# Two state-space layers: scans of one state and two sequences, driven from PSUM, summed by accumulating turns

## The reference

```python
x = silu(conv(in_proj_w @ hidden) + conv_b)        # u: (4, 256 channels, 256 times)
dt_low, B, C = split(x_proj_w @ u, [8, 16, 16])
delta = softplus(dt_proj_w @ dt_low + dt_proj_b)
A = -exp(A_log)                                     # (256, 16 states)
def step(state, (d, b, c, u)):                      # scan over the 256 times
    state = state * exp(d[..., None] * A) + (d * u)[..., None] * b[:, None, :]
    return state, einsum('ben,bn->be', state, c)
y = (ys + D * u) * silu(z)
return swapaxes(y, 1, 2)
```

## Time and profile before

| | |
|---|---|
| median of 3 runs | 2662.31 us (2658.98 to 2666.39) |
| the profiled execution, its own time | 2666.48 us |
| its span, first to last instruction | 2664.5 us |
| PE busy, mean granted clock | 1977.8 us (74%), 0.844 |
| DVE busy | 1610.6 us (60%) |
| ACT busy | 786.8 us (30%) |
| POOL busy | 580.7 us (22%) |
| scans of L795, 32 | 204.2 us |
| multiplications of L790, 64 | 75.2 us |

### The profile page before, as it was taken

One profiled execution on the slowest core, in us unless ns is written; L12 is line 12 of the kernel. 1 busy time (PEld: TensorE's weight loads), 2 busy tenths in 40 slices (PEclk: granted clock), 3 DMA queues, 4 the chain that ended last, 5 costly groups with the idle time before them and its releaser, 6 DMA issues.

```text
span 2664.5 us, 27749 instructions
## 1 busy us (share of the span) xinstructions
PE 1977.8 (74%) x9734; PEld 1251.4 (47%) x9734; DVE 1610.6 (60%) x2456; ACT 786.8 (30%) x1999; POOL 580.7 (22%) x327
## 2 busy tenths in 40 slices
PE   5646668746635776788888864553999999999986
PEld 3522234412222445666666633343566665555743
DVE  4279956879988543555555179998366424444114
ACT  1333302133212025455554011110355314444000
POOL 1314420014501014233332036555000000000000
PEclk9867878768867879888889877876899999999966
DMA  3000020010010210000001100000000100000000
GB/s 102 7 32 0 0 54 3 5 45 0 0 40 1 35 42 2 17 12 12 12 10 50 71 1 0 0 0 0 6 10 10 42 10 13 12 10 21 1 32 16
DMA packets 25727, 48.98 MB, mean 18 GB/s; under 512 B 6262, under 2 KB 19603, under 8 KB 24092
## 3 DMA queue, kind: packets, MB, share of 16 engines
q1 hardware_dynamic: 25644, 47.85, 5.9%
HBM read 42.20 MB, written 1.05 MB: 16 GB/s over the span
## 4 chain that ended last, share of the span: by engine, by line
PE 51%; DVE 37%; ACT 4%; issue 4%; SPq 1%; POOL 1%; DMA 1%; DVEq 0%; ACTq 0%; POOLq 0%
DVE big L795 8%; PE banks L1116 7%; PE banks L1085 7%; PE banks L1125 7%; PE banks L1054 6%; DVE big L1796 5%; PE banks L1108 3%; DVE big L1792 3%; DVE big L495 2%; PE banks L1350 2%; PE banks L417 2%; PE banks L428 2%; DVE big L790 2%; DVE big L776 1%; DVE arena L1172 1%
## 5 line engine op out<-in xcount | busy, mean ns | idle before, releaser
L1191 DVE COPY arena<-banks 128x512 f32<-128x512 f32 x196 | 135.4, 691 | 329.8 <-PE banks L1108 329.5
L218 POOL TENSOR_TENSOR ln_rstd<-ln_var_eps,neg_half 128x2 f32<-128x2 f32 x48 | 36.8, 766 | 1060.8 <-DVE ln_var_eps L206 1060.8
L1085 PE MATMUL banks<-big 128*128 128x256 f32 x784 | 235.6, 413 | 6.0 <-ACT big L1227 4.4
L1116 PE MATMUL banks<-arena,big 128*128 128x256 f32 x784 | 227.7, 414 | 6.3 <-DVE arena L1191 6.3
L1248 ACT ACTIVATE arena<-banks,arena 128x256 f32<-128x256 f32 x392 | 193.0, 499 | 60.8 <-DVE arena L1165 43.0
L795 DVE TENSOR_TENSOR_SCAN big<-big 128x2048 f32<-128x2048 f32 x32 | 204.2, 6380 | 1.1
L707 PE MATMUL banks<-big,ident 128*128 128x512 f32 x288 | 171.3, 749 | 39.2 <-POOL big L868 39.1
L868 POOL TENSOR_TENSOR big<-big 128x2048 f32<-128x2048 f32 x32 | 144.7, 4523 | 252.2 <-DVE big L795 252.2
L1266 ACT ACTIVATE big<-banks 128x256 f32 (+1 forms) x196 | 75.1, 383 | 348.4 <-PE banks L1116 348.4
L1054 PE MATMUL banks<-x_feat,arena 128*128 128x512 f32 x392 | 176.4, 592 | 0.0
L1125 PE MATMUL banks<-arena,big 128*128 128x256 f32 x784 | 174.3, 382 | 1.9 <-ACT big L1266 1.9
(11 more groups left out here) (313 smaller groups left out, 3568.1 us busy)
## 6 DMA issues: line engine op xcount, KB each, us to landing
big<-big SPq DMA_DIRECT2D x32, 64.0 KB, 2.3
arena<-in_L0f_w SPq DMA_DIRECT2D x1, 2048.0 KB, 8.0
arena<-in_L1a_wo SPq DMA_DIRECT2D x1, 2048.0 KB
arena<-in_L1f_gv SPq DMA_DIRECT2D x1, 2048.0 KB
arena<-in_L2a_qk_w SPq DMA_DIRECT2D x1, 2048.0 KB
big<-big SPq DMA_DIRECT2D x64, 32.0 KB
arena<-in_L2x_wo SPq DMA_DIRECT2D x1, 2048.0 KB
arena<-in_L2x_q_w SPq DMA_DIRECT2D x16, 128.0 KB, 2.0
```

The source lines that it names most:

```text
L1085: last = mm(ps[:, h * SEQ:(h + 1) * SEQ], q[:, b * SEQ + h * P:b * SEQ + (h + 1) * P], k[:, b * SEQ:(b + 1) * SEQ], start=True, stop=not s ...
L1116: last = mm(slot, self.v[:, 2 * b + kc, :], self.probs_t[:, u % 2, kc, :], start=(kc == 0), stop=(kc == 1))
L1191: v.tensor_copy(self.probs_t[:, u % 2].rearrange("p a b -> p (a b)"), B[4 + u % 2][:]).then_inc(self.turn_read, 1)
```

## The change

The steps of a state-space layer become 32: one state and two sequences (half the tokens) each, first the 16 states of the first half, then those of the second. They are written out, without a hardware loop.

- PE spreads B into bank 4 and C into bank 5, one bank each. It then adds by turning: eight transposes of 128 x 128 of out, accumulated in banks 6 and 7, which so hold the sum by tokens. With the last state of a half it also turns and adds D * u (sixteen transposes). In its queue, slot s holds spread(s+1) and then add(s-1).
- DVE writes drive into PSUM, banks 0 and 1 or 2 and 3 in turn, 128 x 1024, and scans 128 x 1024 with decay from SBUF and drive from PSUM. Slot s holds drive(s+1) and then scan(s).
- ACT makes the decay with two exponentials of 128 x 510, copies one bank of C, scales u by D in slot 0, and reads the two banks of sums into SBUF (over du) after each half.
- POOL multiplies 128 x 1024. It clears the decay's first times after the softplus, when du is done.
- The gate is no tile any more: the LayerNorms ahead of layers 1 and 4 (those of layers 0 and 3) apply Silu where they copied, so that x_feat holds the gate; DVE multiplies the sums by it, pair by pair, and the next LayerNorm adds from SBUF. These two LayerNorms turn into banks 0 to 3.
- The x_proj matmuls wait for both halves of u and go to banks 4 and 5; dt uses banks 6 and 7 twice.
- SmallHeads (attention of layers 0 and 6) and StateSpace get parameters hosts and room, with which an attention would carry a state-space layer's steps in its own queues. The table of makers, which the diff leaves as it is, passes neither, so hosts is False and room is None everywhere.

The diff, cut to its core (the parts under hosts and the renaming of semaphores left out):

```diff
 class LayerNorm:
+    def turn_bank(self, pair):
+        return pair if self.gates else 4 + pair
...
-            ... e.x_tok[:, ts, :], e.bank[pair][:].rearrange("p (a b) -> p a b", a=2), ALU.add))
+            ... e.x_tok[:, ts, :], self.y(pair).rearrange("p (a b) -> p a b", a=2), ALU.add))
...
-                                 e.bank[4 + pair][:]...., ACT.Copy).then_inc(e.xt_ready, 1)
+                                 e.bank[self.turn_bank(pair)][:]...., ACT.Silu if self.gates else ACT.Copy).then_inc(e.xt_ready, 1)
...
+HALVES = 2
+STEPS = HALVES * STATES
 class StateSpace:
+        halves = lambda ap: ap.rearrange("p (k j t) -> p k j t", j=CH, t=BANK)
+        self.decay = halves(work[:, 0:2 * TOKENS])
+        self.drive = [e.banks[:, 2 * n:2 * n + CH, :] for n in range(2)]
+        self.state, self.out = halves(room[:, 0:2 * TOKENS]), halves(room[:, 2 * TOKENS:4 * TOKENS])
...
+    def tensor_low(self, pe):
+        pe.wait_ge(self.s_u, CH)
...
+    def tensor_spread(self, pe, k):
+        if k == 0:
+            pe.wait_ge(self.s_parts, 2)
+        else:
+            pe.wait_ge(self.s_c_read, k)
+            pe.wait_ge(self.s_driven, k)
+        for n in range(2):
+            last = self.e.nc.tensor.matmul(self.e.bank[4 + n][:], self.pick[0:3 * BC, n * STATES + k % STATES, :], self.parts[0:3 * BC, self.cols(k)], start=True, stop=True)
+        last.then_inc(self.s_bc_psum, 1)
+
+    def tensor_add(self, pe, k):
...
+        elif first:
+            pe.wait_ge(self.s_y_read, k // STATES)
+        pe.wait_ge(self.s_outed, k + 1)
+        sources = [self.out[:, k % 2]] + ([self.u[:, :, self.cols(k)]] if last else [])
+        for src in sources:
...
+            for t in range(4):
+                for j in range(CH):
+                    at = (t % 2) * D + j * P
+                    ins = e.nc.tensor.matmul(e.bank[6 + t // 2][:, at:at + P], src[:, j, t * P:(t + 1) * P], e.ident[:], is_transpose=True,
+                                             start=(first and at == 0), stop=False, skip_group_check=True)
...
+    def tensor_slot(self, pe, s):
+        if s + 1 < STEPS:
+            self.tensor_spread(pe, s + 1)
+        if s:
+            self.tensor_add(pe, s - 1)
...
+    def vector_drive(self, dve, k):
+        dve.wait_ge(self.s_bc_psum, k + 1)
...
+        if k >= 2:
+            dve.wait_ge(self.s_scanned, k - 1)
+        self.e.nc.vector.tensor_tensor(self.drive[k % 2], self.du[:, :, self.cols(k)], bcast(self.e.bank[4][:], 1, CH), ALU.mult).then_inc(self.s_driven, 1)
+
+    def vector_slot(self, dve, s):
+        if s + 1 < STEPS:
+            self.vector_drive(dve, s + 1)
...
+        dve.wait_ge(self.s_decay, s + 1)
+        dve.wait_ge(self.s_driven, s + 1)
+        if s >= 2:
+            dve.wait_ge(self.s_outed, s - 1)
+        flat = lambda ap: ap.rearrange("p j t -> p (j t)")
+        self.e.nc.vector.tensor_tensor_scan(flat(self.state[:, s % 2]), flat(self.decay[:, s % 2]), flat(self.drive[s % 2]), 0.0,
+                                            ALU.mult, ALU.add).then_inc(self.s_scanned, 1)
...
+        for pair in range(4):
+            dve.wait_ge(self.s_y_read, pair // 2 + 1)
...
+            v.tensor_tensor(out, out, e.x_feat[:, :, pair * SEQ:(pair + 1) * SEQ], ALU.mult).then_inc(e.y_ready, 1)
...
-        ch.mark(a(self.gate, e.x_tok[:], ACT.Silu))
...
+    def scalar_step(self, act, k):
...
+            act.wait_ge(self.s_scanned, k - 1)
+        for j in range(CH):
+            seqs = lambda ap: ap.rearrange("p (b t) -> p b t", b=2)[:, :, 1:]
+            last = a(seqs(self.decay[:, k % 2, j, :]), seqs(self.delta[:, j, self.cols(k)]), ACT.Exp, scale=self.a_neg[:, j, n:n + 1])
+        last.then_inc(self.s_decay, 1)
+        act.wait_ge(self.s_bc_psum, k + 1)
+        if k >= 2:
+            act.wait_ge(self.s_outed, k - 1)
+        a(self.c[:, k % 2, :], self.e.bank[5][:], ACT.Copy).then_inc(self.s_c_read, 1)
...
+    def scalar_slot(self, act, s):
+        if s + 1 < STEPS:
+            self.scalar_step(act, s + 1)
...
+        if s % STATES == 1 and s > STATES:
+            self.scalar_y(act, s // STATES - 1)
...
+    def gpsimd_slot(self, pool, s):
+        pool.wait_ge(self.s_c_read, s + 1)
+        pool.wait_ge(self.s_scanned, s + 1)
+        if s >= 2:
+            pool.wait_ge(self.s_added, s - 1)
+        self.e.nc.gpsimd.tensor_tensor(self.out[:, s % 2], self.state[:, s % 2], bcast(self.c[:, s % 2, :], 1, CH), ALU.mult).then_inc(self.s_outed, 1)
...
+            scans = which in (1, 4)
+            blocks.append((l, LayerNorm(e, l, y=blocks[-1][1].y if scans else None, gates=which in (0, 3))))
```

More of the change, by code:

```diff
@@ L327, in sync @@
             sp.dma_start(dst, src).then_inc(self.w_loaded, 16)
+        if self.hosts:
+            self.beside.load(sp)
         e.wait_x_feat(sp, l)
@@ L459, in tensor, with proj_bank, v_bank @@
                 last.then_inc(e.y_ready, 1)
+        if self.hosts:
+            self.beside.tensor_slot(pe, STEPS)
+    def proj_bank(self, blk, s, half):
+        return (0 if blk or self.hosts else 4) + 2 * s + half
+    def v_bank(self, pair):
+        return pair if self.hosts else 4 + pair
     def vector(self, dve):
@@ L545, in scalar @@
         e.wait_x_feat(act, self.l)
+        if self.hosts:
+            self.beside.scalar_in(act)
         for blk in range(2):
@@ L694, in tensor @@
-        pe.wait_ge(self.s_dt_act, 4)
-        for q in range(4):
-            nc.tensor.matmul(B[4 + q][:], self.zero_bf[:, 0:P], self.zero_bf, start=True, stop=False, skip_group_check=True)
-        pe.wait_ge(self.s_dbl_read, 2)
-        def spread(row, banks):
-            for half in range(2):
-                last = nc.tensor.matmul(B[banks + half][:], self.pick[0:3 * BC, bass.ds(row, 1), :].rearrange("p a b -> p (a b)"),
-                                        self.parts[0:3 * BC, half * BANK:(half + 1) * BANK], start=True, stop=True)
-            last.then_inc(self.s_bc_psum, 1)
@@ new lines, in tensor_slot, with tensor, vector_conv @@
+    def tensor_slot(self, pe, s):
[3 more added lines that the diff above has]
+            self.tensor_add(pe, s - 1)
+    def tensor(self, pe):
+        if not self.hosted:
+            self.wait_start(pe)
+            self.tensor_in(pe)
+            self.tensor_low(pe)
+            self.tensor_dt(pe)
+            self.tensor_spread(pe, 0)
+            for s in range(STEPS + 1):
+                self.tensor_slot(pe, s)
+    def vector_conv(self, dve):
+        v, ch = self.e.nc.vector, self.e.dve_chain
@@ L873 @@
+    def gpsimd(self, pool):
+        if not self.hosted:
+            self.wait_start(pool)
+            self.gpsimd_clear(pool)
+            for s in range(STEPS):
+                self.gpsimd_slot(pool, s)
 DH = 128
```

457 lines of the change are left out of this document (257 added, 200 removed).

## The result

The changed kernel takes 2642.5 us (median of 9 runs, 2638.1 to 2650.4), the kernel before on the same chip 2666.4 (9 runs, 2659.0 to 2677.6): a ratio of 0.991, with a 95% interval of 0.989 to 0.992. It is faster by 24 us. The prediction said 2647, with 2605 to 2685. Runs 6 to 10 are single executions, so their windows are read and not their times.

A forecast was written before the change was run, and what follows sets the result against it. The vector engine was taken to bound the state-space loops (285.5 of 2664.5 us). Loops +1.1, tails -13.0, ahead +2.6 and high-clock steps -6.2 gave -15.5 us: median 2662.3 becomes 2647, range 2605 to 2685.

The forecast's parts named there:

- the loops: Both layers' scan loops: 286.6 us against 285.5, +1.1, before -6.2 for the steps at the high clock.
- the tails: From last scan to the LayerNorm's first addition: 8.2 us each, 16.4 against 29.4 for both, -13.0.
- ahead of the loops: First x_proj matmul's two passes come behind the second Silu: 1.3 us a layer, +2.6 in all.
- The bound: Scan loop: unheld scan 2.29 us, vector engine's step 3.58, but spread queued behind add makes TensorE a second loop.
- The hold of 5.13 us: Loop, scan's end to next-but-one drive at low clock: 0.03 + 2.26 + 0.06 + 1.60 + 1.18 us.
- L868's own form is nearer, so 2.26: GpSimd's product of 1024 in the loop: half of 4.52 us, 2.26, bounds 1.9 and 2.36.
- The high clock for a sixth of the steps: Loop, after the half's sixteen turns: a sixth of 62 steps at 3.76 us in place of 4.36, -6.2.
- low clock: TensorE in the new loop mostly at 1.2 GHz, as in the attention stretch: a step of 4.36 us.
- the rival of the high clock: TensorE at 2.4 GHz through the loop: 0.60 us less on 62 steps, 2611 us; chance 0.18.
- The held scan: Loop: scan still held by GpSimd's product, a step of 4.6 us, 2668 us; chance 0.10.
- The dear turns: Loop: accumulating turn costs twice, hold 6.73 us, step 5.16, 2709 us; chance 0.13.
- the dear PSUM operations: Loop: vector instructions writing or scanning PSUM cost more; 0.3 us a step gives +19, 2672 us; chance 0.17.

The follow-up runs named there:

- Runs 6 to 10: Single executions of the changed kernel with c buffers moved (Runs 6 to 9) or x_proj matmuls early (run 10).
- run 2: Changed kernel with TensorE's adds one slot later and four c buffers instead of two: 2600.0 us, 0.973 of the kernel before.
- Runs 1 to 4: Changed kernel with adds one slot later, 2615.0 us; that plus four c buffers, 2600.0; only drive in SBUF, 2653.2; all three edits, 2648.2.
- Runs 6 to 9: Changed kernel with c buffers in the large tile, 2642.2 us; then 14, 256 and 16 words further, 2642.3, 2652.2 and 2663.4 us.
- run 6: Changed kernel with its c buffers laid in the large tile, where the kernel before had them: 2642.2 us, loops 142.6 and 142.7 us.
- run 5: Changed kernel with four matmuls of zeros on TensorE between the spread and the adding turns: 2602.5 us, 0.974 of the kernel before.
- run 10: Changed kernel with each x_proj matmul waiting only for its own half of u: 2649.2 us.
- run 4: Changed kernel with adds one slot later, four c buffers and drive in SBUF again: 2648.2 us, 0.990 of the kernel before.

## Why the prediction was right, and what in it was not

**The size (near in the time, less near in the change).** The time was put at 2647 and is 2642.5. The change was put at -15.5 us and is -24, by its interval -20 to -30. Part of the nearness is the base: the prediction started from a median of 2662.3, of three runs, where nine gave 2666.4. By the windows, with the forecast first: the loops -5.1 and -11.0, the tails -13.0 and -12.6, ahead of the loops +2.6 and +3.2, everywhere else nothing and -4.2. So the loops hold most of what was missed.

**The bound (right).** The scan with one SBUF operand isn't held, 2.28 us for 2.29; and the gain goes into a wait for TensorE, whose queue holds the spread behind the add. The vector engine's own step was put at 3.58 and is 3.52 (drives at 216.22 and 219.74 in run 2). Runs 1 to 4 show both halves apart: having drive in PSUM is worth 22 us a loop when the wait is gone, and 1.8 when it isn't (and 1.75 in each tail).

**The hold of 5.13 us (right in sum, its terms off both ways).** In the timeline it is 5.05: GpSimd starts 0.13 us behind the scan's end (0.03 was put), the turns start 2.05 after that (2.32 with the wake-up), the spread 1.77 after the turns (1.60), and the drive 1.10 after the spread (1.18). The turns' weight loads take 1.57 us, so an accumulating turn costs what a plain one does, 0.20. The largest single miss is GpSimd's product, 2.00 for 2.26. The vector engine's own drive and scan behind the wait take 3.41 us (222.47 to 225.88), not 3.58. A pair of steps is 8.46 where 8.71 was put.

**The loop, per layer.** The prediction had 143.3 us, less 3.1 for a sixth of the steps at the high clock. The pairs give 15 x 0.25 = 3.8 less. The high clock did not come, +3.1: the granted clock is 0.50 for nearly all of the loop, and only around the half it is higher. Windows around the sixteen turns, the first while they run, the second behind them:

```profile
274.00:277.30 3.30, 3.30 (x17) 3.29 (x18) 2.66 (x2) 1.16 (x2) 0.51 (x1) 0.52 0.00 0
277.30:284.00 6.70, 3.82 (x17) 2.36 (x15) 4.17 (x3) 4.01 (x7) 3.49 (x2) 0.75 0.00 0
```

The half cost 1.55 us beyond its pairs (drives at 273.24 and 283.25, 10.01 us for one pair, which is 8.46 elsewhere), where 2.0 was put. The first scan ends 6.62 us after the softplus, not 7.05. And the last scan follows the one ahead directly (the two start at 335.18 and take 4.46 us together, so the last adds 2.2), for there is no drive behind it, where the sum had charged a whole step of 3.58: -1.4. Together 140.2 - 3.8 + 3.1 - 0.45 - 0.43 - 1.4 = 137.2, measured 137.4 and 137.2.

**The mis-sized term** is GpSimd's product, and the step that failed with it is "L868's own form is nearer, so 2.26". Runs 6 to 9 show that the form was not all: with c in the large tile, where the kernel before had it, the product of 1024 takes 2.35, and 14 words further 2.00, as in the changed kernel. The prediction's two bounds, 1.9 and 2.36, were nearly the two cases, and the choice between them was made by size where it hung on an address. With c as in run 6 the two loops are 10.7 us longer and the tails 1.3, half of the change's gain.

**"The high clock for a sixth of the steps" (wrong).** It was a guess from sixteen turns in a row; the clock rose behind them and is 0.50 again from 290 to 339 us. For both layers the shorter pairs are worth -7.6 us and the missing high clock +6.2: the two nearly cancel, and that is luck. The main choice, low clock, was right, and run 5 shows what hung on it: the rival of the high clock, 2611, is near where the run with zero matmuls came out, 2602.5.

**The tails (right).** 16.4 predicted, 16.8 measured. GpSimd and the vector engine hold one another up here as well: the two gates and the product beside them took 3.07 and 2.30 us in place of 1.29 and 2.00, of which only the product's 0.3 is on the path.

**Ahead of the loop (near in size, not in reason).** +2.6 predicted, +3.2 measured. But the two passes brought behind the second Silu cost only 0.54 and 0.09 us (6.77 and 6.29 us against 6.23 and 6.20 before), and taking them out again gave no more than the spread (run 10). And +3.2 is of one profile: in 15 of the 22 stretches with this code the stretch is 55.96 to 55.98 us, where layer 1's is 57.51 here and the kernel before had 55.2 and 55.1. At that value the two layers together would be at +1.6. In layer 1 the matmuls of dt took 6.31 us at a mean granted clock of 0.60 (before: 4.60 us at 0.79), and the first eight of the layer took 6.72 us where 5.33 had been; what made the clock differ there wasn't tried. The Silu's table load of 1.28 us did lie off the path: at 131.85 in layer 0's LayerNorm, whose first copy starts at 138.42.

**The rivals.** The held scan fell (2.28 us always); run 4 is the kernel that it described, with a step of 4.28 us where 4.6 was put. The dear turns and the dear PSUM operations fell (1.57 us for eight turns, 7 ns for a drive). The high clock did not come (0.52 and 0.51 in the loops).

## What to carry to other kernels

When an edit frees the engine that bounds a loop, draw the loop again through the queues of the others: here a step of the old order in TensorE's queue kept 22 of 28 us a layer, and moving one line gave most of it back. A resource conflict that is removed shows little while another wait keeps the two instructions apart, so test it in the version without that wait, too. And when a shape is priced by halving a row of a larger one, look whether the operands' addresses stay what they were.

## What the runs showed of the hardware that was not expected

- GpSimd's product of 128x1024 fp32 with a broadcast operand takes 2.00 or 2.35 us by where that operand starts: in one tile with the other operand, 14 words past a multiple of 512 gives the shorter, 0, 16 and 256 words past it the longer.
- TensorE busy for 26.6 and 26.8 of 40 us was granted 0.50 in one kernel and 1.00 in another, which had four bf16 matmuls of 512 columns more in each step. Work that adds nothing to the output made the kernel 40 us faster. In run 2 it was busy for 30.4 of the same 40 us and had 0.50. Which property of the added matmuls did it, no run here separates.
- Two SBUF operands on the vector engine beside a GpSimd product: a scan that started second lost 0.76 us for 0.89 shared; two gates lost 1.78 us in 2.3; and a product that started second, behind a running scan, took 3.84 us in place of 2.00 while the scan lost nothing.
